# Four-stage transformer kernel on one core: the gates of the first feed-forward block are made of tanh, an add and two multiplies instead of silu

## The reference

```python
x = x + _L0_attn_ref(_layernorm(x), W_qkv)                 # attention, 16 heads of 8
x = x + _L0_ffn_ref(_layernorm(x), w_gate, w_up, w_down)   # the block of the change
x = x + _L1_attn_ref(_layernorm(x), w_qkv, w_out, b_out)   # causal, rotary numerator, plain denominator
x = x + _L1_ffn_ref(_layernorm(x), router_w, w1, w2, bias) # 8 experts, top 2, capacity

def _L0_ffn_ref(x, w_gate, w_up, w_down):                  # H = 128, I = 352
    gate = fp4_linear(x, w_gate)       # fp4_linear rounds both operands to FP4 in blocks of 16
    y = fp4_linear(x, w_up)
    h = jax.nn.silu(gate) * y
    return fp4_linear(h, w_down)
```

## Time and profile before

| | |
|---|---|
| median of 3 runs | 1946.72 us (1943.99 to 1947.26) |
| the profiled execution's own time | 1940.03 us |
| its span | 1938.3 us |
| mean granted clock of PE | 0.95 of full |
| instructions | 33298 |

### The profile page before, as it was taken

The page is one execution under the profiler, slowest core; times in us unless marked ns, Lnnn a source line. Parts: engine busy times, 40 slices in busy tenths (PEclk is TensorE's granted clock), DMA queues, the critical chain, the costliest instruction groups (busy, mean ns, idle before and its releaser), DMA issues. The chain is left out here.

```text
span 1938.3 us, 33298 instructions
## 1 busy us (share of the span) xinstructions
PE 1640.8 (85%) x12863; PEld 631.1 (33%) x12948; DVE 1180.8 (61%) x2110; ACT 1455.6 (75%) x2516; POOL 259.5 (13%) x268
## 2 busy tenths in 40 slices
PE   5489999999999999953788997888889888873995
PEld 3122222222222222232234332433233333222674
DVE  7899999999999998368264544455354533213220
ACT  4167787777787778722999999999999999992221
POOL 4400000000000000042000100010001113321466
PEclk9689999999999999966999999999999999996998
DMA  4300011100000000053111221113012223231433
GB/s 136 124 2 26 30 36 33 32 26 27 26 26 27 26 26 5 2 206 101 63 50 50 72 93 49 50 44 120 19 36 77 93 66 111 95 117 39 138 61 31
DMA packets 68431, 115.85 MB, mean 60 GB/s; under 512 B 9305, under 2 KB 54213, under 8 KB 62640
## 3 DMA queue, kind: packets, MB, share of 16 engines
q1 hardware_dynamic: 58416, 92.87, 15.0%
q0 software_dynamic: 9856, 20.83, 3.8%
HBM read 71.49 MB, written 42.14 MB: 59 GB/s over the span
## 5 line engine op out<-in xcount | busy, mean ns | idle before, releaser
L752 ACT ACTIVATE probs<-psS 128x512 f32<-128x512 f32 x1024 | 556.4, 596 | 187.1 <-PE psS L656 185.6
L771 DVE TENSOR_REDUCE max_of_halves<-psM 128x2 f32<-128x1024 f32 x512 | 617.3, 1222 | 46.2 <-PE psM L625 16.8
L1529 ACT ACTIVATE exps<-cpsS 128x1024 bf16<-128x1024 f32 x512 | 540.7, 1090 | 27.4 <-PE cpsS L1296 26.9
L1296 PE MATMUL cpsS<-rotary_stack 128*128 128x512 bf16 x952 | 289.1, 387 | 79.9 <-ACT exps L1529 30.6
L676 PE MATMUL psO<-probs,plain_v 128*9 128x256 f32 x4096 | 317.0, 381 | 4.9 <-issue 2.2
L1539 ACT ACTIVATE cprobs<-cpsS 128x1024 f32<-128x1024 f32 x256 | 277.7, 1085 | 20.7 <-PE cpsO L1329 17.3
L1276 PE MATMUL cpsS<-rotary_stack 128*128 128x512 bf16 (+3 forms) x755 | 193.0, 331 | 63.1 <-ACT exps L1529 37.4
L625 PE MATMUL psM<-plain_top 64*128 64x512 bf16 x1024 | 211.8, 394 | 31.5 <-DVE max_of_halves L771 22.7
L656 PE MATMUL psS<-plain_top 64*128 64x512 bf16 x1024 | 213.2, 388 | 7.4 <-issue 6.1
L656 PE MATMUL psS<-plain_rest 64*128 64x512 bf16 x1024 | 207.4, 377 | 0.0
L1329 PE MATMUL cpsO<-cprobs,rotary_v 128*9 128x512 f32 (+3 forms) x1536 | 155.1, 492 | 0.6 <-DVE rotary_sums L1855 0.6
(11 more groups left out here) (293 smaller groups left out, 1673.4 us busy)
## 6 DMA issues: line engine op xcount, KB each, us to landing
rotary_stack<-q_parts SPq DMA_DIRECT2D x48, 192.0 KB
rotary_stack<-k_parts SPq DMA_DIRECT2D x48, 192.0 KB
rotary_stack<-q_rot_parts SPq DMA_DIRECT2D x48, 192.0 KB
rotary_stack<-k_rot_parts SPq DMA_DIRECT2D x48, 192.0 KB
tokens_taken<-sent_rows POOLq DMA_DIRECT2D x8, 1036.0 KB, 16.9
plain_top<-q_parts SPq DMA_DIRECT2D x64, 96.0 KB
plain_top<-k_parts SPq DMA_DIRECT2D x64, 96.0 KB
e_x<-tokens_taken SPq DMA_DIRECT2D x8, 518.0 KB, 9.7
```

The costliest lines, as they stand in the source:

```text
L752: act.activation(pr[n % SLOTS_P][:, h, :], psS[u % RING][:, :], ACT.Exp, scale=SCALE).then_inc(s_e, 1)
L771: dve.tensor_reduce(mh[g % 2][:, :, hh, t, kh:kh + 1].rearrange("p e o -> p (e o)"), psM[n % 2][:, :, :], AX.X, ALU.max).then_inc(s_r, 1)
L1296: ins = pe.matmul(to[:, kh, :], q[:, x, y_ * P:(y_ + 1) * P], k[:, x, kh * CH:(kh + 1) * CH], start=True, stop=True)
L1529: act.activation(ex[d % EX][:, :, :], psS[n % 3][:, :, :], ACT.Exp, scale=SCALE, accum_out=den[:, at:at + 1]).then_inc(s_e, 1)
```

## The change

Silu is written as `silu(g) = 0.5 * g * (tanh(g / 2) + 1)`.

- **Batches 1 to 3.** The task `silu` becomes two pairs of tasks, one pair for each half (4 tiles, 128x1408). `bend`: ACT writes tanh(g / 2) of the half into `bent`, which lies in `l_ht`. `blend`: DVE makes `gate = (bent + 1) * gate` with one scalar_tensor_tensor. Both halves use the same `bent`, so bend 1 waits for blend 0. The up product of a tile needs only the blend of its half. The factor 0.5 goes into the up product, which becomes a scalar_tensor_tensor of the same size.
- **Batch 0.** ACT writes tanh of each gate tile into free space of `cprobs` and no longer frees the bank; DVE blends each tile from there and the bank (eight scalar_tensor_tensors of 128x352, new on DVE) and frees it.
- **The plan.** The costs in the planner are 2.0 for a bend and 1.6 for a blend, in place of 6.0 for silu; the places of the tasks behind them move with that.

```diff
@@ middle_tasks @@
-    tasks.append((("silu", n), "other", 6.0, [("g", n, t) for t in range(TB)], 0.0))
+    if n:
+        for c in range(2):
+            tasks.append((("bend", n, c), "other", 2.0, [("g", n, t) for t in range(TB)] + [("blend", n, i) for i in range(c)], 0.0))
+            tasks.append((("blend", n, c), "vector", 1.6, [("bend", n, c)], 0.0))
     for t in range(TB):
-        tasks.append((("u", n, t), "slot", 0.5, [("silu", n)] if n else [("g", n, t)], 0.0))
+        tasks.append((("u", n, t), "slot", 0.5, [("blend", n, t // TC)] if n else [("g", n, t)], 0.0))
@@ late_phase @@
-        act_keeps = label[1] == 0 and label[0] in ("x", "g", "h", "px")
+        act_keeps = label[1] == 0 and label[0] in ("x", "h", "px")
...
+        s_bl, s_bt = sem("gates_blended"), sem("first_gates_bent")
...
+        bent = ht_area[:, 0:TC * I].rearrange("p (t i) -> p t i", i=I)
+
+        def first_bent(t):
+
+            at = 2 * I + 2 * BLOCKS + t % 2 * I
+            return pr[t // 4][:, t // 2 % 2 * 2:t // 2 % 2 * 2 + 2, :, :].rearrange("p h b n -> p (h b n)")[:, at:at + I]
+
+        def blends(n, t):
+
+            return (n - 1) * 2 + t // TC + 1
@@ the scalar engine's work @@
-                if kind == "silu" and n:
+                if kind == "bend":
                     wait_kept(act, ("g", n, TB - 1))
-                    act.activation(gate[:, :, :], gate[:, :, :], ACT.Silu).then_inc(s_si, 1)
+                    if label[2]:
+                        act.wait_ge(s_bl, blends(n, 0))
+                    act.activation(bent, gate[:, label[2] * TC:(label[2] + 1) * TC, :], ACT.Tanh, scale=0.5).then_inc(s_si, 1)
+                elif kind == "g" and n == 0:
+                    act.wait_ge(s_f, use[label] + 1)
+                    act.activation(first_bent(label[2]), bank(label)[:, 0:I], ACT.Tanh, scale=0.5).then_inc(s_bt, 1)
...
-                    elif kind == "g":
-                        act.activation(gate[:, label[2], :], bank(label)[:, 0:I], ACT.Silu).then_inc(s_ka, 1)
@@ the vector engine's work @@
+                elif kind == "blend":
+                    dve.wait_ge(s_si, (n - 1) * 2 + label[2] + 1)
+                    at = slice(label[2] * TC, (label[2] + 1) * TC)
+                    dve.scalar_tensor_tensor(gate[:, at, :], bent, 1.0, gate[:, at, :], ALU.add, ALU.mult).then_inc(s_bl, 1)
...
-                        dve.tensor_copy(gate[:, cc, :], bank(label)[:, 0:I]).then_inc(s_kd, 1)
+                        if n:
+                            dve.tensor_copy(gate[:, cc, :], bank(label)[:, 0:I]).then_inc(s_kd, 1)
+                        else:
+                            dve.wait_ge(s_bt, cc + 1)
+                            dve.scalar_tensor_tensor(gate[:, cc, :], first_bent(cc), 1.0, bank(label)[:, 0:I],
+                                                     ALU.add, ALU.mult).then_inc(s_kd, 1)
                     elif kind == "u":
                         if n:
-                            dve.wait_ge(s_si, n)
+                            dve.wait_ge(s_bl, blends(n, cc))
                         else:
                             wait_kept(dve, ("g", n, cc))
-                        dve.tensor_tensor(gate[:, cc, :], gate[:, cc, :], bank(label)[:, 0:I], ALU.mult).then_inc(s_kd, 1)
+                        dve.scalar_tensor_tensor(gate[:, cc, :], bank(label)[:, 0:I], 0.5, gate[:, cc, :],
+                                                 ALU.mult, ALU.mult).then_inc(s_kd, 1)
```

## The result

The changed kernel took **1933.68 us** (median of 4 runs, 1932.16 to 1935.21); beside it the kernel before took 1946.99 (4 runs, 1943.99 to 1947.53). The ratio is 0.9935 [0.9918, 0.9952]: faster by some 13 us, where 10.0 was forecast. The time lies 3.0 us under the forecast of 1936.7 and inside the range. In the three sets of experiments the kernel before had medians of 1941.3 to 1942.4, so that absolute times there are lower, and each is compared with the kernel before of its own set.

A forecast was written before the change was run, and what follows sets the result against it. ACT was taken to set the pace from 919 to 1758 us, with DVE's work counting in the lead. Terms -8.5 - 2.0 + 0.5 = -10.0 us took the median of 1946.72 to 1936.7, range 1932.5 to 1942.5.

The forecast's parts named there:

- Two bends cost 2.46 us: ACT's stream in batches 1 to 3: two bends take 2.46 us (at most 3.0) in place of silu's 5.3.
- The term of -8.5: ACT's stream among the units: three silus replaced by bends save 8.5 us, 6.9 at the lower bound.
- What the pause costs beyond itself: Behind the silus, PE's clock falls and ACT waits for scores; removing this saves 2.0 us (0 to 2.5).
- The blends: DVE among the units: six blends of about 1.6 us stay hidden under exponentials and PE's lead, costing nothing.
- The lead: Before the units: table loads there are worth nothing; batch 0's last blend delays DVE's first up product, +0.5 us.
- The moved tasks: Rounding, head merging and routing of batch 0 change places but run in DVE's free half, costing nothing.
- One of the prediction's own signs of being wrong: Among the units: new waits for PE's scores appearing behind the up products would show the prediction wrong.
- clock term: Behind the silus: PE's clock stays up with shorter pauses and ACT's waits for scores go, saving 2.0 us.
- Rival A: Blends among the units run at half speed, about 3.0 us each; +1.0, giving 1937.7 us; chance 0.18.
- Rival B: Every new scalar_tensor_tensor is slow, batch 0's too: +4.7 instead of +0.5 there, giving 1940.9 us; chance 0.06.
- Rival C: PE waits 1 us too long at the up products' bank per batch, no clock gain: 1941.7 us; chance 0.12.
- Rival D: ACT stands at bend 1 for 6.6 us per batch behind a pair's rounding on DVE: 1956.7 us; chance 0.04.

The follow-up runs named there:

- tanh_for_silu: Kernel before with tanh in place of silu everywhere, in one piece of 2816 columns, blends left out, old task order: 1932.03 us, ratio 0.9951 to before.
- old_plan: Changed kernel with all tasks at their places of before, bends and blends set in around silu's old place: 1929.66 us, ratio 0.9935 to before.
- rest_later: Changed kernel with batch 1's second down product and the tasks following it moved 2.4 places later (last three 1.0): 1928.11 us, ratio 0.9928 to before.
- silu_in_bends: Changed kernel with silu in place of tanh in the six bends, so twelve table loads return: 1950.57 us, ratio 1.005 to before.
- down_later: Changed kernel with only batch 1's second down product and its close followers put back near their old place: 1935.32 us, ratio 0.9967 to before.
- blend_twice: Changed kernel with each of the six blends among the units made twice: 1932.39 us, ratio 0.9955 to before.
- lead_only: Kernel before with only batch 0's part of the change, batches 1 to 3 keeping silu: 1940.42 us, ratio 0.9995 to before.
- lead_silu: Changed kernel with batch 0's gates again silu on ACT, with two table loads and no blends there: 1930.17 us, ratio 0.9946 to before.
- before_again: Kernel before, unchanged, profiled a second time: span 1940.7 us, unit stage 836.5 us.

## Why the prediction was right

The account of the units closes to 0.6 us in five kernels from two readings, stops and waits (us, against the first profile of the kernel before, whose stops are 15.9 and waits 36.3):

| kernel | stops | waits | sum | units measured |
|---|---|---|---|---|
| the change | -8.4 | -1.7 | -10.1 | -10.3 |
| `tanh_for_silu` | -8.6 | -1.2 | -9.8 | -10.1 |
| `old_plan` | -8.3 | -3.2 | -11.5 | -11.9 |
| `rest_later` | -8.4 | -4.4 | -12.8 | -12.9 |
| `silu_in_bends` | +8.9 | -2.5 | +6.4 | +5.8 |

- **Two bends cost 2.46 us.** Measured 2.53 (1.26 and 1.27). The slope of 0.85 ns for a further column, from an exponential and a silu, holds for tanh, and the gap of 0.15 that stood around the silu isn't there around a bend. The term of -8.5 came out as -8.4.
- **What the pause costs beyond itself, -2.0.** Right in kind, too small, and read from half of its rows. The waits behind the silus of before were 3.54 us: the earlier trace rows has 0.59 and 1.69, but 0.60 behind batch 1's (at 975.28), which the prediction said has no such wait, and 0.66 at 1392.05 were missed. In the change there is none behind the six bends: -3.5 (-3.3 against the second profile of before). `tanh_for_silu` shows where they come from: where the clock stayed at 1.00 the wait is gone, and where it fell to 0.50 it is there to 0.01 us, at half the pause. No run changed the clock by itself; that the slow clock makes PE late is the reading that fits all these places, with scores that take 1.03 us in place of 0.60, and `down_later` shows the same where no silu is near. `silu_in_bends` puts a condition on it: three slow stretches there were followed by no wait. And `blend_twice` shows that a wait at these places can also come at full clock, when the up products are late; in the change they weren't.
- **The blends, 0.** They took the 1.6 us forecast, no bend waited for one, and twice the blends cost 1.7 us in ACT's waits behind the gates and 1.4 to 2.4 in the units. The cover is real and has an end near the 1.3 us that were counted for batch 2: with 1.63 us more, ACT waited 0.49 there, so 1.1 us were to spare.
- **The lead, +0.5.** DVE's first up product came 6.14 us behind the first tanh (forecast: 6.2; 5.90 and 5.61 in the other two profiles), and some 0.4 later than before over all profiles, with a scatter as large. That it "passes through" is not shown: the lead as a whole takes 92.1 to 92.95 us in the change and 92.2 and 93.65 before, and `lead_only` with 0.9995 [0.9986, 1.0004] can't be told from zero. In `lead_silu` the lead with two table loads is as long as in the change, 92.8 us, so they cost at most some tenths.
- **The moved tasks, 0.** This term failed. One of the prediction's own signs of being wrong came true with it, in part: there are new waits for PE's scores behind the up products of batch 3, though at the down products and not at the bank. The prediction looked at DVE, POOL and SP for what the planner moved, and said that it runs in DVE's free half. What cost something moved on PE: a down product of 3.1 us ahead of a sum for which ACT waits, 3.50 us in place of 1.11. The other shifts, about 1 us each and of both signs, took part of it back. Together the moved order cost 1.8 us in this profile (-3.5 behind the gates, -1.7 in all waits), and 0.9 and 1.1 in the other two. It hid the larger clock term: the sum of -1.7 lies close to the -2.0 forecast. That the sum was met so closely is in part two errors that cancel, which is luck.
- **Profile and median.** The three profiles of the change give -10.3, -10.8 and -11.2 in the units; the medians give -13.3, -12.0 and -9.8, whose intervals all hold these. What the first two have above it is not explained by a stage: `before_again` removes the suspicion that the profile of before was quick there.
- **The range.** Its low end, 1932.5, is 3.6 us under the best sum of 1936.1, and not "part of" the 2.7 us of spread that it names. With all of the 2.7 it would be 1933.4, and 1933.68 would still lie inside.

**Rival A (blends at half speed)** is out: the 1.01 ns for each further column between the tensor_tensors of the earlier trace rows, 892 for 704 and 1216 for 1024, gives 1605 for 1408, and 1626 was measured. The Trainium skill, "Vector Engine (DVE) Microarchitecture Reference", section 7, has half throughput for this form with two SBUF sources that are not bf16; by it a blend would be about 3.0 us, an estimate. The trace doesn't agree, and the measurement decides. **Rival B** is out with it: 520 to 522 ns for each of batch 0's blends. **Rival C (new waits of PE at the bank, no clock term)**: the clock term came in full, and the new waits came by the order of tasks at the down products, not by the bank behind the blends. Its path is real, though, and comes with blends twice as long (`blend_twice`). Its price of 3.0 us in all is more than the 0.9 to 1.8 that the new waits cost, and for the wrong place. **Rival D (ACT stands at bend 1)** did not come: no wait at any of the six bends.

## What to carry to other kernels

A function outside the table of the engine's main function costs two loads and the pause of everything fed by that engine; count the waits behind the pause by looking at each place, not only at the two largest. When the costs in a planner change, compare the order of the engine that releases the bound one (here PE's sums and scores, not only DVE's free time), and repair the plan by moving the whole train of tasks: moving one alone was dearer than leaving it, since PE then stood for rows that weren't ready and lost its clock too.

## What was not expected of the hardware

- PE's granted clock did not follow the length of its pause alone. In the kernels with tanh it stayed at 1.00 (2.4 GHz) behind pauses of up to 1.33 us in the change and of 1.70 and 1.86 us in `tanh_for_silu`, and fell to 0.50 (1.2 GHz) behind one of 2.75. But behind batch 3's first bend of `old_plan` it fell, 0.67 over 5 us, after only 1.57 us, and behind batch 1's second bend of `silu_in_bends` it stayed at 1.00 after 2.87. What else decides is open.
- A fallen clock need not cost anything: `silu_in_bends` had it behind three bends with no wait of ACT. Nor is the wait in proportion to the slow stretch: behind batch 1's silu the clock was low for about 7 us in the kernel before and for about 3.5 in `lead_only`, with a pause of PE of 4.55 us in both, and ACT waited 0.60 and 0.48 us.
- A table load took 1283 ns each time. A bend with its two loads takes 4.13 us of ACT's stream, without them 1.26: 1.43 per load, as (5.3 - 2.45) / 2 gives for the silu of 2816. The Trainium skill, "ScalarE: Activation LUTs", section "What ACT_TABLE_LOAD costs", has 1283 ns and a drain of some 1380 behind it for each switch. The first figure is the trace's, the second isn't seen in this stream.
- Tanh cost what silu did: 2.54 to 2.60 us for 2816 columns beside 2.55 in the earlier trace rows, and it needed no table load between exponentials.
